# Expert lists split by rank, with the token's sum forwarded through two rounds of scatters

## The reference: two expert layers around an attention by FFT

```python
def ffn(x, router_w, router_bias, sw1, sw3, sw2, ew1, ew2):
    xf = x.reshape(-1, C)
    shared_out = jax.nn.silu(xf @ sw1) * (xf @ sw3) @ sw2            # hidden 512
    s = sigmoid(xf @ router_w.T)                                     # 8 experts
    _, topk_idx = jax.lax.top_k(s + router_bias, 2)
    s_sel = take_along_axis(s, topk_idx, axis=1)
    denom = s_sel.sum(axis=1, keepdims=True)
    gates = where(denom > 1e-09, s_sel / (denom + 1e-09), 1.0 / 2)
    comb = einsum('nke,nk->ne', one_hot(topk_idx, 8), gates)
    h = gelu(einsum('nd,edh->neh', xf, ew1), approximate=False)      # hidden 256
    y = einsum('neh,ehd->ned', h, ew2)
    return shared_out + einsum('ned,ne->nd', y, comb)

def attn(x, Wq, Wk, Wv):
    q, k, v = (einsum('bsd,ed->bse', x, W) for W in (Wq, Wk, Wv))
    fk, fq = rfft(k) / (abs(rfft(k)) + 1e-8), rfft(q) / (abs(rfft(q)) + 1e-8)
    return x + irfft(cumsum(fk * rfft(v), axis=-2) * conj(fq), n=D)

x = x + 0.5 * ffn(layernorm(x), ...)
x = x + attn(layernorm(x), ...)
x = x + 0.5 * ffn(layernorm(x), ...)
```

## Time and profile before

| | us |
|---|---|
| median of 3 runs | 2051.76 (2050.72 to 2052.6) |
| the profiled execution | 2060.44 |
| its span | 2058.6 |

### The profile page before, as it was taken

One profiled execution on the slowest core, in us unless ns is written; L12 is line 12 of the kernel. 1 busy time (PEld: TensorE's weight loads), 2 busy tenths in 40 slices (PEclk: granted clock), 3 DMA queues, 4 the chain that ended last, 5 costly groups with the idle time before them and its releaser, 6 DMA issues.

```text
span 2058.6 us, 35171 instructions
## 1 busy us (share of the span) xinstructions
PE 1597.5 (78%) x9854; PEld 1381.3 (67%) x9855; DVE 1419.2 (69%) x3362; ACT 672.2 (33%) x1126; POOL 766.7 (37%) x868
## 2 busy tenths in 40 slices
PE   2899999589999466767767674489999976999940
PEld 1777777489999355555555563377777766999940
DVE  4788888545555368888898888377788763555557
ACT  3334343134444133232323131233433412444410
POOL 0444444225454223333333232044444432555420
PEclk9999999889999767776777676599999987999975
DMA  8211111144444301010101000011111114444459
GB/s 276 82 53 42 55 50 47 53 120 143 140 142 135 96 22 41 21 41 20 41 20 41 20 20 0 31 54 51 45 50 55 42 44 114 140 138 143 136 194 349
DMA packets 123782, 170.36 MB, mean 83 GB/s; under 512 B 14881, under 2 KB 105394, under 8 KB 123442
## 3 DMA queue, kind: packets, MB, share of 16 engines
q1 hardware_dynamic: 89938, 91.05, 15.5%
q0 software_dynamic: 25344, 70.29, 9.3%
q10 hardware_dynamic: 8448, 8.39, 1.2%
HBM read 91.03 MB, written 81.89 MB: 84 GB/s over the span
## 4 chain that ended last, share of the span: by engine, by line
PE 47%; DVE 18%; issue 12%; DMA 10%; POOL 7%; ACT 3%; SPq 2%; POOLq 0%; DVEq 0%; ACTq 0%
PE bank L613 14%; PE bank L614 12%; PE bank L615 12%; POOL lists L407 6%; DMA lists<-a_rows,a_slots 5%; PE bank L739 3%; PE bank L749 3%; DVE t_rn L1149 2%; DMA f_yf<-results 2%; DVE t_cum L1167 2%; ACT a_rows L503 2%; DVE a_gate_u L987 1%; PE bank L843 1%; DVE X L1230 1%; DVE t_pr L1165 1%
## 5 line engine op out<-in xcount | busy, mean ns | idle before, releaser
L418 POOL DMA_INDIRECT results<-b_yb,b_goal x272 | 261.6, 962 | 343.6 <-DVE b_yb L1090 298.4
L407 POOL DMA_INDIRECT lists<-a_rows,a_slots x256 | 259.8, 1015 | 117.5 <-issue 64.5
L613 PE MATMUL bank<-t_xah,t_wfh 128*128 128x512 f32 x192 | 115.0, 599 | 113.6 <-DVE t_xal L864 64.1
L1090 DVE COPY b_yb<-bank 128x512 f32<-128x512 f32 x136 | 94.0, 691 | 147.9 <-PE bank L615 147.9
L613 PE MATMUL bank<-a_sw2h,a_uh 128*128 128x256 f32 x512 | 155.4, 304 | 42.7 <-DVE a_xtl L864 35.7
L613 PE MATMUL bank<-ew_h,b_xbth 128*128 x544 | 166.7, 306 | 1.1 <-DVE b_xbtl L864 1.0
L613 PE MATMUL bank<-ew_h,b_hth 128*128 x544 | 155.9, 287 | 7.5 <-DVE b_htl L864 3.0
L457 ACT ACTIVATE a_uh<-a_gate_u 128x512 fp32r<-128x512 f32 x128 | 77.1, 624 | 245.9 <-PE bank L615 193.0
L614 PE MATMUL bank<-ew_l,b_xbth 128*128 x544 | 154.1, 283 | 0.0
L615 PE MATMUL bank<-ew_h,b_xbtl 128*128 x544 | 153.8, 283 | 0.0
L615 PE MATMUL bank<-ew_h,b_htl 128*128 x544 | 152.4, 280 | 0.0
(11 more groups left out here) (212 smaller groups left out, 4882.2 us busy)
## 6 DMA issues: line engine op xcount, KB each, us to landing
b_xb<-lists SPq DMA_DIRECT2D x272, 132.0 KB
t_yg<-results SPq DMA_DIRECT2D x32, 512.0 KB, 4.6
f_yf<-results SPq DMA_DIRECT2D x32, 512.0 KB, 10.9
X<-in_L_attn_x SPq DMA_DIRECT2D x16, 512.0 KB, 4.1
out<-X ACTq DMA_DIRECT2D x16, 512.0 KB, 7.1
results<-b_yb,b_goal POOLq DMA_INDIRECT x272
w_raw_ew<-in_L_ffn_ew SPq DMA_DIRECT2D x2, 2048.0 KB, 13.8
lists<-a_rows,a_slots POOLq DMA_INDIRECT x256, 2.4
```

What stands on the lines that cost most here:

```text
L407: pool.indirect_dma_start(out=lists, out_offset=bass.IndirectOffsetOnAxis(ap=slots[:, q, k, j:j + 1], axis=0), in_=rows[:, q, j, :], in_of ...
L418: pool.indirect_dma_start(out=results, out_offset=bass.IndirectOffsetOnAxis(ap=goal[:, slot, blk:blk + 1], axis=0), in_=YB[:, slot, blk, : ...
L613: pe.matmul(o, a("h"), b("h"), start=first, stop=False)
L1090: dve.tensor_copy(YB[:, slot].rearrange("p b d -> p (b d)"), bank[:, 7 - par, :]).then_inc(s_yok, 1)
```

## The change

There are now sixteen lists, eight for a token's first choice (the chosen expert of lower number) and eight for its second; both halves of `lists` have a twin `base` of the same places. Phase A scatters the updated row of `X` to its first slot in `base`, four more DMAs per chunk, and each list row carries the token's second slot, both gates and the token's number. Phase B runs in two rounds of 35 pairs. Round one computes gate times y, adds the row of `base` at the same place, and scatters the sum to `base` at the second slot; round two does the same and scatters to the token's place, in `sums` after the first layer and in the output after the second. Rows beyond a list's end have a goal that is out of range and are dropped. Attention loads `sums` straight into `X`; the combine, the tail's loads and ACT's stores are gone. The diff, cut to its core:

```diff
+LISTS = TOPK * E
+RB = TILES + E - 2
+BLOCKS = TOPK * RB
 PAIRS = BLOCKS // 2
+HALF = PAIRS // 2
...
-        lists = nc.dram_tensor("lists", (E * CAP + E * P, ROW), F32, kind="Internal").ap()
-        results = nc.dram_tensor("results", (2 * TOKENS + 2 * E * P, D), F32, kind="Internal").ap()
+        lists = nc.dram_tensor("lists", (TOPK * RS, ROW), F32, kind="Internal").ap()
+        base = nc.dram_tensor("base", (TOPK * RS, D), F32, kind="Internal").ap()
+        sums = nc.dram_tensor("sums", (TOKENS, D), F32, kind="Internal").ap()
...
-            sp.dma_start(lists[E * CAP:E * CAP + E * P, :], fill[E * P:2 * E * P, :]).then_inc(s_spare, 16)
+            for r in range(TOPK):
+                sp.dma_start(lists[r * RS + E * CAP:(r + 1) * RS, :], c_fill).then_inc(s_spare, 16)
+                sp.dma_start(base[r * RS + E * CAP:(r + 1) * RS, :], c_fill[:, 0:D]).then_inc(s_spare, 16)
...
-                for e in range(E):
-                    end = sp.value_load(table[0:1, 2 * BLOCKS + e:2 * BLOCKS + e + 1], min_val=e * CAP,
-                                        max_val=e * CAP + TOKENS)
-                    sp.dma_start(lists[bass.ds(end, P), :], fill[e * P:(e + 1) * P, :]).then_inc(s_tail, 16)
-                sp.wait_ge(s_tail, E * 16 * (layer + 1))
-                sp.wait_ge(s_spare, 16)
+                for i in range(LISTS):
+                    end = sp.value_load(table[0:1, 2 * BLOCKS + i:2 * BLOCKS + i + 1], min_val=0,
+                                        max_val=(TOPK - 1) * RS + (E - 1) * CAP + TOKENS)
+                    sp.dma_start(lists[bass.ds(end, P), :], c_fill[0:P, :]).then_inc(s_tail, 16)
+                sp.wait_ge(s_tail, LISTS * 16 * (layer + 1))
+                sp.wait_ge(s_spare, 64)
                 sp.wait_ge(s_scat, 2 * J * 16 * CH * (layer + 1))
+                sp.wait_ge(s_base, J * 16 * CH * (layer + 1))
...
+                    if inside(n, PAIRS):
+                        atleast(sp, s_yok, n + (p0 - 3) if not isinstance(n, int) or n >= 4 else 0)
+                        for blk in range(2):
+                            sp.dma_start(XB[:, slot, blk, :], lists[rows_of(n, blk), :]).then_inc(s_xb[slot], 16)
+                    if inside(n - LAG, PAIRS):
+                        if isinstance(n, int) and n == LAG:
+                            sp.wait_ge(s_base_tail, LISTS * 16 * (layer + 1))
+                        if isinstance(n, int) and n == HALF + LAG:
+                            for i in range(4):
+                                sp.wait_ge(s_ysc[i], YW[i] * layer + 32 * ((HALF - i + 3) // 4))
+                        back = (slot - LAG) % 4
+                        for blk in range(2):
+                            sp.dma_start(BB[:, back, blk, :], base[rows_of(n - LAG, blk), :]).then_inc(s_bb[back], 16)
+
+                run_steps(sp, step, 0, 4, HALF - 3, HALF + LAG + 3, 4)
+                run_steps(sp, step, HALF + LAG + 3, HALF + LAG + 3, PAIRS - 2, PAIRS + LAG, 4)
...
+            def load_sums(c, par, half):
+                sp.wait_ge(s_x[par], half * 16 + 16 * CH // 2)
+                sp.dma_start(X[:, bass.ds(c * J, J), :], sums_d[:, bass.ds(c * J, J), :]).then_inc(s_x[par], 16)
+
+            run_steps(sp, load_sums, 0, 2, 2, 2, 2)
...
-            def load_results(c, par, half):
-                atleast(sp, s_comb, c)
-                for k in range(2):
-                    sp.dma_start(YG[:, k, :, :], res_d[:, k, bass.ds(c * J, J), :]).then_inc(s_yg, 16)
-
-            run_steps(sp, load_results, 0, 2, CH, CH, 2)
...
-            def load_last(c, slot, q):
-                atleast(sp, s_fc, c - 3)
-                for k in range(2):
-                    sp.dma_start(YF[:, slot, k, :, :], res_d[:, k, bass.ds(c * J, J), :]).then_inc(s_f[slot], 16)
-
-            sp.wait_ge(s_yok, 2 * PAIRS)
-            run_steps(sp, load_last, 0, 4, CH, CH, 4)
...
+                    if inside(s - 1, CH):
+                        pool.wait_ge(s_xout, s * 2 + 2 * g0)
+                        apart(pool)
+                        for j in range(J):
+                            pool.indirect_dma_start(
+                                out=base, out_offset=bass.IndirectOffsetOnAxis(ap=slots[:, 1 - par, 0, j:j + 1], axis=0),
+                                in_=X[:, (s - 1) * J + j, :],
+                                in_offset=None).then_inc(s_base, 16)
...
+                        atleast(pool, s_scat, g * 128)
+                        pool.wait_ge(s_xn, g + 1)
+                        ch.link(pool.tensor_copy(rows[:, q, :, D + 3:D + 4], tok[:, bass.ds(c * J, J)].unsqueeze(2)))
+                        pool.wait_ge(s_gated, g + 1)
                         pool.wait_ge(s_slot, g + 1)
+                        ch.settle()
+                        apart(pool)
...
-                            out=results,
-                            out_offset=bass.IndirectOffsetOnAxis(ap=goal[:, slot, blk:blk + 1], axis=0),
-                            in_=YB[:, slot, blk, :], in_offset=None).then_inc(s_ysc[slot], 16)
-
-                run_steps(pool, step, 0, 4, PAIRS, PAIRS, 4)
+                            out=to, out_offset=bass.IndirectOffsetOnAxis(ap=goal[:, slot, blk:blk + 1], axis=0),
+                            in_=YB[:, slot, blk, :], in_offset=None, bounds_check=limit - 1,
+                            oob_is_err=False).then_inc(s_ysc[slot], 16)
...
+                act.wait_ge(s_table, layer + 1)
+                for i in range(LISTS):
+                    end = act.value_load(table[0:1, 2 * BLOCKS + i:2 * BLOCKS + i + 1], min_val=0,
+                                         max_val=(TOPK - 1) * RS + (E - 1) * CAP + TOKENS)
+                    act.dma_start(base[bass.ds(end, P), :], c_fill[0:P, 0:D]).then_inc(s_base_tail, 16)
...
-            def store(c, par, half):
-                act.wait_ge(s_fc, c + 1)
-                act.dma_start(out_d[:, bass.ds(c * J, J), :], X[:, bass.ds(c * J, J), :]).then_inc(s_store, 16)
-
-            run_steps(act, store, 0, 2, CH, CH, 2)
...
-                    ch.link(dve.tensor_copy(inc_b[:, 0].rearrange("p e j -> p j e"), msk))
-                    ch.link(dve.tensor_copy(slotv.rearrange(flat).rearrange("p (e j) -> p j e", e=E), msk))
                     ch.link(dve.tensor_tensor_scan(cnt.rearrange(flat), res_e, msk.rearrange(flat), 0.0,
                                                    ALU.mult, ALU.add))
                     ch.settle()
+                    ch.link(dve.scalar_tensor_tensor(pick2[:, 0], cnt, 1.0, msk, ALU.is_equal, ALU.mult))
+                    ch.settle()
+                    ch.link(dve.tensor_tensor(pick2[:, 1], msk, pick2[:, 0], ALU.subtract))
+                    ch.settle()
+                    ch.link(dve.tensor_copy(by_list.rearrange("p (k e) j -> p k j e", k=TOPK), pick2))
+                    ch.link(dve.tensor_copy(inc_b[:, 0].rearrange("p (k e) j -> p k j e", k=TOPK), pick2))
+                    ch.settle()
                     dve.tensor_tensor_scan(inc_b[:, 1].rearrange("p e j -> p (e j)"), res_j,
-                                           slotv.rearrange(flat), 0.0, ALU.mult, ALU.add).then_inc(s_mask, 1)
-
-                def gate(c):
-
-                    ch.settle()
-                    for k in range(TOPK):
-                        ch.link(dve.tensor_tensor(prod2[:, k], pick2[:, k], prob[:], ALU.mult))
+                                           by_list.rearrange("p l j -> p (l j)"), 0.0, ALU.mult,
+                                           ALU.add).then_inc(s_mask, 1)
...
+                def gate(c, par):
+
+                    ch.link(dve.tensor_tensor(prod2, pick2, bc(prob[:].unsqueeze(1), [P, TOPK, J, E]), ALU.mult))
...
+                    both = gsum[:, 0:2 * J].rearrange("p (k j) -> p k j", k=2)
+                    ch.link(dve.tensor_tensor(both, both, bc(gsum[:, 16:20].unsqueeze(1), [P, TOPK, J]), ALU.mult))
+                    ch.settle()
+                    dve.tensor_tensor(rows[:, par, :, D + 1:D + 1 + TOPK].rearrange("p j k -> p k j"), both,
+                                      bc(gsum[:, 20:24].unsqueeze(1), [P, TOPK, J]), ALU.add).then_inc(s_gated, 1)
...
                 def places(c, par):
 
 
                     g = c + g0
-                    ch.link(dve.scalar_tensor_tensor(pick2[:, 0], cnt, 1.0, msk, ALU.is_equal, ALU.mult))
-                    ch.settle()
-                    ch.link(dve.tensor_tensor(pick2[:, 1], msk, pick2[:, 0], ALU.subtract))
-                    ch.settle()
+                    dve.wait_ge(s_gated, g + 1)
...
+                    ch.link(dve.tensor_copy(rows[:, par, :, D], few[:, 8 + J:8 + 2 * J]))
+                    atleast(dve, s_base, (g - 1) * 64)
...
                         hidden(s + 1, 0)
+                        gate(s + 1, 1 - par)
                         places(s + 1, 1 - par)
                         hidden(s + 1, 1)
                     if far:
                         dve.wait_ge(s_xh, s + (g0 + 3))
```

(25 more changed lines are left out.)

186 lines of the change are left out of this document (84 added, 102 removed).

## The result

The changed kernel takes 2272.03 us (median of 4 runs, 2268.03 to 2278.65), the kernel before 2051.24 beside it (2046.23 to 2052.6); the ratio is 1.1076, with a 95% interval of 1.1052 to 1.1100. Run again later, on a chip of its own group, it was 2270.53 against 2051.73, ratio 1.1051 (1.1021 to 1.1082). The profiled execution has a span of 2276.8 us, 218.2 more than before.

A forecast was written before the change was run, and what follows sets the result against it. TensorE was taken to bound phase B, with SP's loads replacing it, and TensorE and a DVE chain in turn phase A. Phase B 145 + phase A 103 + table 25 + start 9 - attention 6 - tail 72 = +204: 2256 us, range 2200 to 2310.

The forecast's parts named there:

- the likeliest case: Whole kernel: the main forecast of 2256 us, own range 2200 to 2310, chance 0.70.
- Attention, -6: Attention: removing the combine only turns work into wait; a gain at the entry alone, -6 us, a rough figure.
- tail: End of kernel: the last scatter ends the run near 1986.5 instead of 2058.6, -72 us.
- the step on the lead: Phase B: releasing XB only after y needs 4.2 us per pair, less than SP's 4.7, so it does not decide.
- The round boundary: Phase B at pair 35: SP waits for round one's scatters to issue and land, 4.5 us, bounds 2 and 8.
- the moved gate: Phase A: gate ahead of a_xtl on DVE adds 2.1 us per chunk, 63 us over 30 chunks.
- the fall: Phase A: TensorE's longer stand drops its clock in 22 more chunks, 1.8 us each, +40 us.
- Table and filler rows: Between phases A and B: sixteen filler writes instead of eight and a longer table, +12.3 us per layer, both +25.
- The gate's move covered: Rival, phase A: an earlier a_rows brings DVE's chain forward, so phase A stays as it is; 2153 us, chance 0.13.
- The clock in phase B: Rival, phase B: TensorE's stands drop the clock in each pair, 112 us more; 2368 us, chance 0.09.
- The slow table read: Rival, phase B: each table read takes 0.578 us, 168 us more on SP; 2424 us, chance 0.02.
- Busy time alone: Rival, whole kernel: stages are bound by busy time, not order; -78 us, 1974 us, chance 0.06.

The follow-up runs named there:

- two more table reads: Changed kernel with two more reads of a row number per pair on SP, results unused; 2398.29 us, ratio 1.1679.
- small base rows: Changed kernel with only 16 of the 256 columns of each base row loaded and added; 2273.10 us, ratio 1.1055.
- SP's reads taken away: Changed kernel with a pair's row numbers kept in SP's registers, two table reads less per pair; 2223.82 us, ratio 1.0824.
- the lead and the kept numbers: Changed kernel with row numbers kept in registers and the gate column copied out, so b_xb is released before y; 2120.39 us, ratio 1.0339.
- its repetition: The changed kernel run once more, unchanged; 2270.53 us, ratio 1.1051.
- gate last: Changed kernel with gate put back behind a_xtl on DVE; 2316.62 us, ratio 1.1126.
- gate on POOL: Changed kernel with gate computed on POOL ahead of the list scatters, instead of on DVE; 2260.39 us, ratio 1.0867.
- the combine alone in the kernel before: Kernel before the change without the combine's multiply-adds in attention, loads kept; 2045.07 us, ratio 0.9965.
- the statistics: Changed kernel with DVE's statistics moved between the adds of the down projection's first and second half; 2268.93 us, ratio 1.1062.
- the doubled matmuls: Changed kernel with TensorE doing the first half of the down projection twice in each chunk; 2414.93 us, ratio 1.1625.

## Why the prediction was right, and where not

**The verdict and the size** hold: slower by more than 10%, 2272 against 2256, inside the likeliest case's own range. The sum is nearer than its terms: phase B was 37 us too low, phase A 18 and the table 6 too high, so that the total is off by only 14 is partly luck. Three of the six terms are right to 1.5 us (start, attention, tail). The tail's gain of 71.5 us is real; beside it only attention gains.

**Phase B, +145 forecast, +182 measured.** The step "four loads of 1.17 us on SP become the bound" is shown: 1.17 us apart in the trace, time follows SP's work (two more table reads), not bytes (small base rows). Two parts were mis-sized. First, the step on the lead: "12 us of later steps: 16.7/4 = 4.2 us, less than 4.7, so it does not decide". It took the steps behind the load as fixed microseconds. They are three periods of the pipeline; with 5.2 us from y to the transposes, 4p = 5.2 + 2.9p gives p = 4.7 us, and with SP's reads taken away 4.63 was measured. The 2.9 is read from one pair, and with 3.0 the same sum gives 5.2: so the sum only shows that the ring is about as long as SP's work, and the figure to keep is the measured one. It does decide, together with SP. That two bounds of one size, each with its own variation, make 5.0 us and not 4.7 is argued, not shown. Second, TensorE gained 0.35 us in nearly every pair in which the profile shows nothing it waits for (20.0 us in 58 of 70). It comes where the expert numbers are read from the table; that these reads are its cause is not shown. With the lead and the kept numbers it is down to 1.3 us in five waits, so it goes with TensorE being late and may be a part of the ring; it wasn't tried by itself.

**The round boundary, 4.5 us forecast** as added wait: the interval there is 9.4 us in layer 0 and 9.1 in layer 1, 4.5 and 4.1 more than the mean of the others. Right, though the 2.5 us taken for a landing read as 2.2 from its rows (419.13 less 415.78 and 1.10). The bounds check on the scatters, for which nothing was taken, costs nothing to speak of: 0.985 us each (L438) against 0.962.

**Phase A, +103 forecast, +85 measured.** The ring of before and after gives 1.6 us per chunk for the moved gate (forecast 2.1) and 1.5 for the fall (forecast 1.8, in 22 more chunks; the stand is 2.9 us in each chunk read, not 3.4). That is the mechanism as forecast, with both terms a little too large. The clock's term has a second witness in the intervals with 6.8 us of low clock, 1.2 us longer than those with 3.4. But the split is read from the trace, and not proved by undoing: with gate last the stage was slower still, since the rows that carry gates are scattered only behind the gate; with gate on POOL 1.2 us of the 3.1 came back before POOL became the bound. How much a free gate would give back is open.

**Attention, -6.** Measured -5 in the change (-10.6 in its repetition), and -5.5 for the combine alone in the kernel before. The multiply-adds on an engine busy 85% of the stage cost next to nothing, 5.5 of 58 us: shown by the wait that took their place.

**Table and filler rows, +25 forecast, +18.6 (22 in the repetition).** Sixteen filler writes take 20.31 us, (20.31 - 0.33)/15 = 1.33 each, against 1.36 from the earlier trace rows. The 1.4 us more per layer for the table itself are not there: from the last slots to the first filler write are 29.1 and 30.6 us, before 30.3 and 30.0. The rest of the difference is open.

```profile
456.44 20.31 SPq L334 DMA_DIRECT2D lists<-in_c_fill  x16
```

**The rivals.** The gate's move covered (2153): refuted by the stand of 2.9 us and the 24.4 us a chunk. The clock in phase B (2368): refuted, 1.00 from 509 to 670 us at a busy share of 0.84, with stands of 0.2 to 1.7 us; it fell behind one stand of 2.25 us at the start and behind the boundary's. The oscillation that the Trainium skill ("TensorE: Matmul & The Clock Gate", HAM oscillation) describes doesn't occur at stands up to 1.7 us here. The slow table read (2424): refuted; in phase B of layer 0 a read takes 0.269 us as the median and 0.517 at most. The Trainium skill ("DMA: Bandwidth & Descriptors", Latency and other measured facts) has a floor of about 600 ns; the trace doesn't agree, its longest read is under it and its median less than half of it. Busy time alone (1974): refuted by SP's 1.17 us a load and by the combine.

```profile
L342 SPq TENSOR_LOAD <-table x263: 262/269/517, 500.7 to 830.2; - x132
```

## What to carry to other kernels

A transfer whose row is computed at run time costs its issuing engine 1.17 us here, half of it for fetching the row number; count these before bytes, and keep a number in a register if it is used twice. When a buffer's release is moved to the end of a software pipeline, write the latency as periods: depth x period = fixed part + stages x period. A bound found that way can hide behind another of the same size, so one removed alone proves little. Busy time taken off an engine that then only waits for another comes back as wait: 52 of the 58 us of the combine did, and all of the 2 us a chunk of the statistics. And an engine that takes over work can become the bound itself, as POOL did with the gate.

## What was not expected of the hardware

- In the run with the doubled matmuls, 72 matmuls back to back, the engines that wait for the last one went on 3.7 us after its recorded end in the chunk read (1.1 to 5.4 in 26 of the 32 chunks). Its cause is open.
- On the second group's chip phase B of the same code took 7 to 17 us longer in each layer than on the others, and the kernel before 1.3 to 1.4% longer over all: differences of a per cent between groups of runs say nothing without the kernel before beside them.
